# Graph and mixture-of-experts kernel, one core: weight splits moved from the second relational aggregation into the three graph layers

## The reference, cut to what matters

```python
x = x + L0_gnn(layernorm(x))     # two relational layers: per-edge messages summed over 40000 edges
x = x + L0_ffn(layernorm(x))     # first mixture: 8 experts, top 2, 256 -> 1024 -> 256
x = x + L1_gnn(layernorm(x))     # three graph layers (width 256, 256, 128), then a projection
x = x + L1_ffn(layernorm(x))     # second mixture: 8 experts, top 2
# a graph layer, with A the matrix of edge counts between nodes:
h = relu(dinv * (A @ (dinv*h@W)) + h@W * deg_inv + b)
```

## Time and profile before

| what | before |
|---|---|
| median of 3 runs | 2290.3 us (2288.63 to 2292.11) |
| profiled execution, its own time | 2286.1 us |
| its span, first to last instruction | 2284.2 us |
| mean granted TensorE clock | 0.914 |
| first aggregation, 186 to 632 | 446 us |
| second aggregation, 632 to 1097 | 465 us |
| routing and experts of the first mixture, 1097 to 1477 | 380 us |
| transform, 1477 to 1526 | 49 us |
| graph layer 0, 1526 to 1654 | 128 us: PE busy 117.9, ACT 63.7, DVE 70.1 |
| graph layer 1, 1654 to 1779 | 125 us: PE busy 117.3, ACT 54.9, DVE 60.3 |
| graph layer 2, 1779 to 1854 | 75 us: PE busy 66.9, ACT 34.5, DVE 46.8 |
| routing and experts of the second mixture, 1854 to 2284 | 430 us |

### The profile page before, as it was taken

How to read it: one execution, slowest core, us unless ns; L and a number is a source line. 1 busy time by engine, 2 the same in 40 slices (tenths; PEclk the granted TensorE clock), 3 DMA queues, 4 the chain that set the end, 5 groups by cost and what they waited for, 6 DMA issues and landing times. The chain is left out here.

```text
span 2284.2 us, 37277 instructions
## 1 busy us (share of the span) xinstructions
PE 1880.0 (82%) x10428; PEld 1570.1 (69%) x10428; DVE 1213.1 (53%) x2759; ACT 1001.3 (44%) x2229; POOL 933.3 (41%) x877
## 2 busy tenths in 40 slices
PE   5995688778858778877499999669899864999996
PEld 3883576567735555555489999558788854899996
DVE  6331122212168888883655555365554565666663
ACT  1555456546455556555033333245444421233332
POOL 0115777777267777776033433220000000334332
PEclk9997889989979999999599999889999965999998
DMA  4894666665358655654544442247664556424262
GB/s 156 350 369 164 229 223 205 238 210 206 130 199 327 212 195 194 202 187 164 206 125 153 98 123 42 56 143 251 233 221 170 171 223 244 122 40 125 41 193 39
DMA packets 127195, 410.00 MB, mean 179 GB/s; under 512 B 21012, under 2 KB 60928, under 8 KB 108544
## 3 DMA queue, kind: packets, MB, share of 16 engines
q1 hardware_dynamic: 56848, 185.62, 22.1%
q0 software_dynamic: 48096, 106.74, 18.1%
q10 hardware_dynamic: 22032, 114.96, 13.3%
HBM read 256.77 MB, written 150.47 MB: 178 GB/s over the span
## 5 line engine op out<-in xcount | busy, mean ns | idle before, releaser
L2231 PE MATMUL ps<-ring,halves 128*128 x3384 | 579.3, 326 | 12.5 <-SPq L2193 4.8
L2231 PEld LDWEIGHTS ps<-ring,halves 128*128 128x128 f32 x3384 | 486.4, 192 | 54.9 <-issue 14.2
L1429 POOL DMA_INDIRECT ring<-tab_rel_next,gidx_relation x313 | 344.1, 1099 | 138.2 <-issue 94.8
L1111 POOL DMA_INDIRECT relation_rest<-tab_rel,gidx_relation x313 | 310.2, 991 | 105.5 <-issue 95.1
L2340 ACT ACTIVATE x_all<-ps 128x512 f32<-128x512 f32 x188 | 113.0, 601 | 455.4 <-PE ps L2250 455.4
L1186 PE MATMUL ps<-relation_rest,slots 128*128 x784 | 215.7, 423 | 97.3 <-SPq L1026 93.4
L1888 PE MATMUL ps<-node_rows,blocks 128*128 128x512 f32 (+1 forms) x1200 | 256.5, 364 | 0.4 <-ACT blocks L1770 0.4
L1186 PEld LDWEIGHTS ps<-relation_rest,slots 128*128 128x128 f32 x784 | 161.4, 211 | 137.3 <-issue 110.3
L1521 PE MATMUL ps<-ring,slots 128*128 x784 | 196.7, 397 | 66.4 <-SPq L1306 40.6
L1888 PEld LDWEIGHTS ps<-node_rows,blocks 128*128 128x128 f32 x1200 | 201.6, 193 | 30.7 <-ACT blocks L1770 0.7
L1521 PEld LDWEIGHTS ps<-ring,slots 128*128 128x128 f32 x784 | 146.9, 196 | 101.6 <-issue 82.4
(11 more groups left out here) (281 smaller groups left out, 2778.7 us busy)
## 6 DMA issues: line engine op xcount, KB each, us to landing
ring<-split_weights SPq DMA_DIRECT2D x12, 4096.0 KB, 14.7
split_weights<-relation_rest ACTq DMA_DIRECT2D x32, 1024.0 KB, 7.1
slots<-tab_counts SPq DMA_DIRECT2D x40, 640.0 KB, 4.0
tab_rel<-relation_rest SPq DMA_DIRECT2D x20, 1024.0 KB, 5.7
tab_rel_next<-relation_rest ACTq DMA_DIRECT2D x20, 1024.0 KB, 4.2
relation_rest<-in_ffn_units ACTq DMA_DIRECT2D x16, 1024.0 KB, 5.1
ring<-split_weights SPq DMA_DIRECT2D x8, 2048.0 KB, 10.0
split_weights<-ring ACTq DMA_DIRECT2D x16, 1024.0 KB
```

Of the source, the lines that this page charges most:

```text
L1111: nc.gpsimd.indirect_dma_start(rows[:, s * wide:s * wide + D], None, table, bass.IndirectOffsetOnAxis(ap=gidx[:, t:t + 1], axis=0)).then_i ...
L1429: nc.gpsimd.indirect_dma_start(rows[:, s * D:(s + 1) * D], None, table, bass.IndirectOffsetOnAxis(ap=gidx[:, t:t + 1], axis=0)).then_inc(g ...
L2231: ins = nc.tensor.matmul(to, lhs[left], weights(slot, right, at, n), start=first and (left, right) == (0, 0), stop=last and left == 1)
```

## The change

The eight units that the second aggregation split (16 to 23) are now pieces of the graph layers. With the 32 pieces that were there already, that makes 64 pieces: 26 in layer 0, 26 in layer 1, 12 in layer 2 (`PIECES`). So that a tile can hold up to two, there are two slots per tile, and `pieces_at` spreads the pieces over the 40 slots evenly. The first slot lies behind `low_half` on ScalarE and behind `whole_row` on VectorE; the second is the old one. The second aggregation loses its copies, subtractions, loads and stores of units.

```diff
+PIECES = (26, 26, 12)
@@ aggregate_and_gate
-                load_unit(0)
@@ ScalarE, per group
-                    u = g // LATESTEP
-                    if u < units:
-                        if g % LATESTEP == LATESTEP // 2:
-                            unit_to_high(u)
-                        if g % LATESTEP == LATESTEP // 2 + 1:
-                            store_unit(u)
-                        if g % LATESTEP == LATESTEP - 1 and u + 1 < units:
-                            act.wait_ge(unit_stored, 32 * (u + 1))
-                            load_unit(u + 1)
@@ VectorE, per group
-                    if g % LATESTEP == LATESTEP // 2 and g // LATESTEP < units:
-                        unit_to_low(g // LATESTEP)
@@ node_layer
-            first_piece = layer * TILES
-            pieces = max(0, min(TILES, UNITS // 2 * 4 - first_piece))
+            first_piece, pieces = sum(PIECES[:layer]), PIECES[layer]
+            def pieces_at(i, half):
+                return range((2 * i + half) * pieces // (2 * TILES), (2 * i + half + 1) * pieces // (2 * TILES))
@@ SyncE, per tile
-                        if i + 1 < pieces:
-                            load_piece(i + 1)
-                        if i < pieces:
-                            store_piece(i)
+                        for k in range(2):
+                            for n in pieces_at(i, k):
+                                if n + 1 < pieces:
+                                    load_piece(n + 1)
+                                store_piece(n)
@@ ScalarE, per tile
                         low_half(b)
+                        for n in pieces_at(b, 0):
+                            high_piece(act, n)
...
                         turned_high(b)
-                        if b < pieces:
-                            high_piece(act, b)
+                        for n in pieces_at(b, 1):
+                            high_piece(act, n)
@@ VectorE, per tile
                         whole_row(b)
+                        for n in pieces_at(b, 0):
+                            low_piece(dve, n)
...
                         turned_low(b)
-                        if b < pieces:
-                            low_piece(dve, b)
+                        for n in pieces_at(b, 1):
+                            low_piece(dve, n)
```

More of the change, by code:

```diff
@@ L75 @@
 LATE = 2 * RING * 2
-LATESTEP = 11
 UNITSTEP = 10
 PIECE = UNITW // 4
+PIECES = (26, 26, 12)
 STEPS = 5
@@ L237, in ring_memory @@
             self.count_work = self.big[:, RINGROWS * D:RINGROWS * D + COUNTWORK]
-            self.late_unit = [self.big[:, RINGROWS * D + COUNTWORK + k * UNITW:RINGROWS * D + COUNTWORK + (k + 1) * UNITW] for k in range(2)]
-            at = RINGROWS * D + COUNTWORK + 2 * UNITW
+            at = RINGROWS * D + COUNTWORK
             self.first_logits = self.big[:, at:at + TILES * E]
@@ L1265, in aggregate_and_gate @@
         with self.stage_block() as (block, sem):
-            onehot_ready, landed, consumed, summed, added, emptied, unit_high, unit_low = sem(
-                "onehot_ready", "landed", "consumed", "summed", "added", "emptied", "unit_high", "unit_low")
+            onehot_ready, landed, consumed, summed, added, emptied = sem(
+                "onehot_ready", "landed", "consumed", "summed", "added", "emptied")
             link, degree, rooted, squared = sem("link", "degree", "rooted", "squared")
             places_ready, src_hot, pair_hot, count_full, bank_out = sem("places_ready", "src_hot", "pair_hot", "count_full", "bank_out")
-            unit_in, unit_stored, kept = sem("unit_in", "unit_stored", "kept")
+            kept = sem("kept")
             variance, row_rooted, rows_ready, turned, hT_ready, logits_full, logits_out, padding_stored = sem(
@@ L1274, in aggregate_and_gate @@
             strip_stored = [sem(f"strip_stored{s}") for s in range(2)]
-            raw, high = self.late_unit
             work = self.count_work
@@ L1283, in aggregate_and_gate @@
             half = KEYS // 2
-            first_unit, units = UNITS, LATE // 2
             gathers = self.gathered
@@ L1331, in _ @@
             def _(act):
[L1332 to L1344, removed]
                 def take_counts(k):
@@ L1406, in _ @@
                             work_on(b)
-                    u = g // LATESTEP
-                    if u < units:
-                        if g % LATESTEP == LATESTEP // 2:
-                            unit_to_high(u)
-                        if g % LATESTEP == LATESTEP // 2 + 1:
-                            store_unit(u)
-                        if g % LATESTEP == LATESTEP - 1 and u + 1 < units:
-                            act.wait_ge(unit_stored, 32 * (u + 1))
-                            load_unit(u + 1)
-                act.wait_ge(unit_stored, 32 * units)
                 act.wait_ge(padding_stored, 16)
@@ L1443, in add @@
                     v.tensor_tensor(to, to, self.ps[g % SUMBANKS][:, 0:D], ALU.add).then_inc(added, 1)
-                def unit_to_low(u):
-                    dve.wait_ge(unit_high, u + 1)
-                    v.tensor_tensor(raw.bitcast(F32R), raw, high.bitcast(F32R), ALU.subtract).then_inc(unit_low, 1)
                 def count_hots(k):
@@ L1733, in store_piece @@
                     sp.dma_start(to[:, 1, :], self.piece_raw[n % 2]).then_inc(piece_stored[n % 2], 16)
-                if pieces:
-                    load_piece(0)
+                load_piece(0)
                 with self.when(sp, True):
@@ L1755, in _ @@
                     move.sync(sp)
-                for k in range(2 if pieces else 0):
+                for k in range(2):
                     sp.wait_ge(piece_stored[k], 32 * (pieces // 2))
```

## The result

| | before | after |
|---|---|---|
| median of the runs | 2289.5 us (4) | 2328.15 us (4; 2325.3 to 2331.8) |
| ratio, 95% interval | 1 | 1.0169 [1.0153, 1.0185] |
| profiled execution | 2286.1 us | 2328.7 us, span 2326.7 |

The changed kernel is slower by 38.7 us. The direction was forecast; the 2307 us and the range up to 2325 were not met.

What follows compares the result with a forecast made beforehand. The gather stream was taken to bound the second aggregation, TensorE layer 0, with VectorE last at layer 2's `multiply`. Terms -11.9 + 9.6 + 9.0 + 1 + 9 = +16.7 us gave 2307.0 us, range 2291 to 2325.

Steps and rivals of the forecast that it cites:

- Second aggregation, -11.9: Second aggregation: without the eight subtractions the eight long gathers shorten to the median, -11.9 us; bounds nothing to 18.3.
- the collision: Second aggregation: each 2.29 us VectorE subtraction holds up a GpSimd gather; eight long gathers last 19.5 us against 7.65.
- The rival in which VectorE paces the stage (-31.5): Second aggregation: VectorE sets the pace, so all 31.5 us freed count; 2287.4 us, no change; chance 0.10.
- the one in which the collision is none: Second aggregation: subtractions do not lengthen gathers, or counting work takes the same port time; +28.6, 2318.9 us; chance 0.10.
- The chain of 4.3 us and the pairs: Layers 0 and 1: copies at least 4.3 us apart; six second-slot-then-first-slot pairs per layer stall TensorE 1.6 or 1.5 us each.
- Layers 0 and 1, +9.6 and +9.0 and 1 for landing: Layers 0 and 1: six stalls each, +9.6 and +9.0 us, plus 1 us for slow store landings; bounds nothing to 38.
- The layers' ends cost nothing: Ends of layers: layer 0 already ends on such a piece; elsewhere its stores land about as engines leave; no cost.
- After each the queues have caught up: Layers 0 and 1: after each pair the queues recover before the next piece, since the following slot is empty.
- Layer 2, +9: Layer 2: 12 new pieces delay engines 3.6 + 3.6 us and strips add 2.1; rounded to 9, bounds 3.6 to 15.
- The late strips: Layer 2: strip loads issued behind a second-slot piece's store come 1.7 us late, pushing `turned_high` by 0.7; +2.1 us.
- Landing stretches: Layers 0 and 1: more pieces bring typical store landing near 4.1 us; +34.9, 2325 us; chance 0.12.
- The pieces are hidden: Graph layers: pieces fit idle time and the 4.3 us is met, leaving only the gathers' gain; 2278.4 us; chance 0.09.

Runs made afterwards that it cites:

- experiment 2: Kernel before, with the second aggregation's eight subtractions cut to one column, copies, loads and stores kept: 2276.6 us, ratio 0.9924.
- experiment 1: Changed second aggregation with the layers of the kernel before (20, 12, 0 pieces; splitting of units 16 to 23 left out): 2279.0 us, ratio 0.9945.
- experiment 9: Kernel before, changed kernel, and changed aggregation with before's layers, repeated on one more chip: 2289.8, 2324.9 and 2277.2 us (last ratio 0.9946).
- experiment 5: Changed kernel with four raw and two high-part buffers, loads two pieces ahead, same 64 pieces: ratios to before 1.0015, 1.0013 and 1.0046.
- experiment 7: Changed kernel with 20, 20, 12 pieces, old slot only, 12 pieces left out: ratios to before 1.0059 and 1.0025.
- experiment 3: Changed kernel with a second high-part buffer, so a copy waits for the stores of the piece before the last: 2326.1 us, ratio 1.0155.
- experiment 6: Changed kernel with the next tile's strip load issued ahead of the second slot's store on SyncE: ratios to before 1.0133 and 1.0129.
- g10: Changed kernel with four raw and two high-part buffers, loads two pieces ahead, and early strip loads, pieces left at 26, 26, 12: ratio to before 1.0.
- 32, 32, 0 version: Changed kernel with four raw and two high-part buffers, early strip loads and 32, 32, 0 pieces: ratios to before 0.9985, 0.9991 and 0.9997.
- e4: Changed kernel with 26, 26, 0 pieces, the last 12 left out: 2316.2 us, ratio to before 1.0105.
- e8: Changed kernel with 20, 20, 12 pieces, old slot only, 12 pieces left out, on a slower chip: ratio to before 1.0059.
- f8: Repeat of e8's kernel (20, 20, 12 pieces, old slot only) on another slower chip: ratio to before 1.0025.
- e1: Changed second aggregation with the layers of the kernel before (20, 12, 0 pieces): 2279.0 us, ratio 0.9945.
- e9: First run of the 32, 32, 0 version, with more buffers and early strip loads, on a slower chip: ratio to before 0.9985.
- e7: Changed kernel with the next tile's strip load issued ahead of the second slot's store, on a slower chip: ratio to before 1.0133.
- f7: Repeat of e7's kernel with the early strip loads on another slower chip: ratio to before 1.0129.

## Why the prediction was right in direction and wrong in size

- **Second aggregation, -11.9.** Right: the collision explains it (experiment 2), and the whole kernel gains 11.6 to 14.7 us from it (experiments 1 and 9). In the first profile of the changed kernel it shows only in part, 7.6 us less of gathers and 5.2 less ahead of the layers; in the second 12.9 and 11.9. The rival in which VectorE paces the stage (-31.5) and the one in which the collision is none both fall. The Trainium skill, "SBUF — State Buffer", section "Who interferes with whom", infers that a `tensor_tensor` does not hold up descriptor generation; experiment 2 contradicts that for these gathers, with 11.0 us.
- **The chain of 4.3 us and the pairs.** Right in place and mechanism: 4.29 us, and stalls at `multiply` in tiles 2, 5, 8, 12, 15 and 18. Experiments 5 and 7 show it, each by taking the chain away. What the prediction put down to the high-part buffer alone is two closed paths; opening one changed nothing (experiment 3).
- **Layers 0 and 1, +9.6 and +9.0 and 1 for landing: the step that failed.** Measured +16.0 and +19.6. The prediction priced a stall of TensorE at its own length, so that busy time stayed as it was; that term was put at nothing without a reason. (a) Missing, and the largest part of the miss: behind some of the stalls the clock is granted at half for some microseconds. The same products take 4.7 and 8.3 us longer, of which the low clock accounts for 11.4 in all, and experiment 5 shows that this goes with the stalls. (b) Idle time grew by 10.3 and 11.7 us where 19.6 was forecast for both together, 2.4 us more. "The layers' ends cost nothing" was wrong: TensorE stands 1.9 and 2.5 us longer at the ends of layers 0 and 1, with two pieces in the last tile. (c) The price of the pairs was near: by its matmuls TensorE stands 9.8 us in the six of layer 0 and 9.3 in those of layer 1. By the weight loads, which the prediction's sign names, it is 12.3 and 11.8 us, with landing 2.9 us in the median and 4.1 at worst. "After each the queues have caught up" was wrong too, since 16 of 26 copies waited.
- **Layer 2, +9: mis-sized in its parts.** The pieces on the engines were put at 7.2 us, and 5.0 and 7.1 us are left without the strips' waits (experiment 6): near. The late strips were put at 2.1 and are 6.2 to 8.3: the landing of a strip was taken as 3.8 us and became 5.4 under the pieces' transfers, with waits up to 3.8 us instead of 1.7.
- **Landing stretches (2325, chance 0.12)** came nearest to the number. Its mechanism is there, but in smaller size, 2.9 instead of 4.1 us; that its number is near is luck, since the time was made up by the clock, the layers' ends and layer 2. *The pieces are hidden* is false as built and true with enough buffers: g10's layers 0 and 1 stand 1.1 and 2.0 us over those of the first profile.
- **Sum.** -11.9 + 9.6 + 9.0 + 1 + 9 = +16.7 forecast. From the first pair of profiles: -5.2 + (10.3 + 4.7) + (11.7 + 8.3) + (13.2 + 0.8) = +43.8, the windows being rounded to whole microseconds, against 42.6.

Open: whether the 32, 32, 0 version beats the kernel before on a chip where gathers don't wait for buffers. Working from the runs, its layers cost 129.4 + 127.4 + 63.8 - 315.2 = 5.4 us and the aggregation gives back some 12, so I estimate 2283 us; it was only run on the other chips, where it was level. Not separated either is what on those chips makes the aggregations longer, and what besides a stall's length decides whether the clock falls.

## What to carry to other kernels

Before you move small pieces of work into "free" time of an in-order engine, walk the whole ring that a buffer goes through (load, copy, subtraction, store, landing, and the order in the queue that issues them) and compare it with the shortest distance between two uses. If it doesn't fit, count all the paths that close the ring, since one more buffer on one of them may buy nothing. Price a stall of a bound TensorE at its length and what the clock takes behind it (here busy time grew by 13 us on top of 22 of idle time, and by 10 in the repeat), look at the last tile of each stage by itself, and take landing times under the load that the change itself makes, not from the quiet line of before.

## What the runs showed of the hardware that was not expected

- A 2.47 us stall of TensorE, after it had been busy at a granted clock of 1.00, was followed by 0.50 and 0.61 for 4 us; a 2.82 us stall was followed by a first `dense` half of 3.45 us instead of 2.41. In another execution a stall of 2.45 us was followed by such a fall and one of 3.66 us was not.
- The second store of a piece (256 KB) landed in 2.5 us in the median before and 2.9 after; the 640 KB strips of layer 2 in 3.8 and 5.4 us, and in 3.8 again where the changed kernel has no pieces in that layer (e4).
- On three chips the kernel before took some 2445 us instead of 2290, and the others were as much longer, all of the difference ahead of the layers. Where two kernels share what they do in a layer, the layer took about the same time on both kinds of chip: 127.0 and 125.0 us (e8), 127.2 and 126.6 (f8) beside 127.2 and 125.2 (e1), 63.8 (e9) beside 63.5 (e4); and, with only the order of a strip load changed, 143.8 and 143.1 (e7), 145.7 and 142.5 (f7) beside 142.7 and 144.8 (after).
